# Queries and keys turned unsplit, four heads at once, and placed by DMAs

## The reference

```python
q = einsum('bsh,oh->bso', x, Wq).reshape(b, s, 16, 32)   # 16 query heads, 4 key/value heads, 32 wide
q = q * cos + rotate_half(q) * sin                       # the same for k
k, v = repeat(k, 4), repeat(v, 4)                        # 4 query heads share one key head
attn = softmax(einsum('bhqd,bhkd->bhqk', q, k) * scaling)
out = einsum('bhqk,bhkd->bhqd', attn, v)                 # then Wo
```

## Time and profile before

| | |
|---|---|
| median of three runs | 1792.23 us |
| profiled execution, its own time | 1810.5 us |
| its span, first to last instruction | 1808.7 us |
| mean granted clock of TensorE | 0.970 |
| busy, share of the span | PE 94%, DVE 59%, POOL 55%, ACT 48% |
| DVE, ACT and POOL from 800 to 900 us | 95.45, 88.94 and 90.05 us of 100 |

### The profile page before, as it was taken

How to read it: one execution, slowest core, us unless ns; L and a number is a source line. 1 busy time by engine, 2 the same in 40 slices (tenths; PEclk the granted TensorE clock), 3 DMA queues, 4 the chain that set the end, 5 groups by cost and what they waited for, 6 DMA issues and landing times.

```text
span 1808.7 us, 25064 instructions
## 1 busy us (share of the span) xinstructions
PE 1694.1 (94%) x8596; PEld 1348.5 (75%) x8596; DVE 1067.5 (59%) x1766; ACT 859.3 (48%) x1274; POOL 1001.0 (55%) x775
## 2 busy tenths in 40 slices
PE   6999999999987989999999999888999899999997
PEld 5887899899865766666666666556888689999885
DVE  4554322222567679999999999997645422222226
ACT  4322222232223348898989898873432212232220
POOL 3115574337433439898989899951221519541645
PEclk9999999999988989999999999999999899999998
DMA  9205553333540000000000000003101535533427
GB/s 344 85 28 214 200 182 129 122 121 125 178 131 24 1 1 1 1 1 1 1 1 1 1 1 1 7 18 143 53 1 47 195 122 175 178 123 105 153 87 233
DMA packets 54310, 160.01 MB, mean 88 GB/s; under 512 B 6704, under 2 KB 7600, under 8 KB 51632
## 3 DMA queue, kind: packets, MB, share of 16 engines
q1 hardware_dynamic: 41360, 84.74, 13.4%
q0 software_dynamic: 12832, 73.67, 11.6%
HBM read 102.29 MB, written 55.84 MB: 87 GB/s over the span
## 4 chain that ended last, share of the span: by engine, by line
PE 61%; DVE 17%; ACT 7%; DMA 7%; issue 6%; POOL 1%; SPq 0%; ACTq 0%; DVEq 0%; another core or an unknown queue 0%; POOLq 0%
PE PS L1051 10%; PE PS L1052 10%; PE PS L1053 10%; DVE nmf L1816 5%; DVE Ph L1833 5%; PE PS L1246 4%; DMA xn<-x_routed 3%; ACT Ph L1529 3%; DMA xs<-x_routed 2%; ACT PT L1522 2%; PE PS L1173 2%; PE PS L1178 2%; PE PS L1176 2%; PE PS L1175 2%; PE PS L1177 2%
## 5 line engine op out<-in xcount | busy, mean ns | idle before, releaser
L1980 POOL TENSOR_TENSOR Pl<-PT,Ph 128x1024 fp32r<-128x1024 f32 x176 | 437.4, 2500 | 78.5 <-ACT Ph L1529 73.4
L1816 DVE TENSOR_REDUCE nmf<-PS 128x1 f32<-128x1024 f32 x256 | 307.8, 1213 | 38.7 <-PE PS L1246 36.0
L1522 ACT ACTIVATE PT<-PS 128x1024 f32<-128x1024 f32 x256 | 259.0, 1016 | 19.9 <-DVE Pl L1839 10.3
L1279 PE MATMUL PS<-Ph,V 128*65 128x512 f32 x512 | 207.4, 405 | 10.3 <-DVE Pl L1839 9.9
L1280 PE MATMUL PS<-Pl,V 128*65 128x512 f32 x512 | 203.2, 397 | 0.0
L1529 ACT ACTIVATE Ph<-PT 128x1024 fp32r<-128x1024 f32 x184 | 194.1, 1055 | 1.5
L1888 POOL TENSOR_TENSOR W<-raw,W 128x544 fp32r<-128x544 f32 x144 | 190.1, 1355 | 1.5
L1246 PE MATMUL PS<-KS,QS 96*128 96x512 f32 x512 | 171.4, 416 | 16.3 <-ACT PT L1522 11.7
L1798 DVE TENSOR_TENSOR thid<-thid,PS 128x352 f32<-128x352 f32 x78 | 40.7, 521 | 245.8 <-ACT thid L1445 245.8
L1264 PE MATMUL PS<-QS,KS 98*128 98x512 f32 x512 | 174.8, 423 | 6.0 <-DVE nmf L1816 5.8
L1445 ACT ACTIVATE thid<-PS 128x352 f32<-128x352 f32 x78 | 36.3, 465 | 260.3 <-PE PS L1178 260.3
(11 more groups left out here) (184 smaller groups left out, 4133.1 us busy)
## 6 DMA issues: line engine op xcount, KB each, us to landing
raw<-ffn_w POOLq DMA_DIRECT2D x18, 2176.0 KB, 10.4
y_routed<-ytile SPq DMA_DIRECT2D x78, 256.0 KB, 2.0
xn<-x_routed SPq DMA_DIRECT2D x40, 256.0 KB, 3.2
...
```

The lines of the kernel that those rows point to most:

```text
L1279: e.matmul(PS[0:VCOL, ob, :], V[:, b * QT + kt, g, :], high_part(u)[:, js], start=kt == 0, stop=False)
L1522: e.activation(PT[:, u % PTBUF, :], PS[:, i:i + 2, :].rearrange("p b n -> p (b n)"), ACT.Exp, scale=SCALE).then_inc(p_ready.sem, 1)
L1816: e.tensor_reduce(nmf[:, (n % 3) * REP + h, t:t + 1], PS[:, i:i + 2, :].rearrange("p b n -> p (b n)"), AX.X, ALU.max, negate=True).then_in ...
L1980: e.tensor_tensor(low_part(u)[:], PT[:, u % PTBUF, :], high_part(u)[:], ALU.subtract).then_inc(pl_pool.sem, 1)
```

## The change

Keys and queries are no longer stacked before they are turned. One transpose takes a rotated tile as it is, all four heads at once (128 tokens by 4 x 32 features), and leaves it unsplit in PSUM; four tiles fill a bank of 512 columns. Then ACT copies the bank as high part (128x512) and VectorE subtracts it as low part, and twelve DMAs on SP (four heads, three rows of the stack, 32 partitions by 512 columns, 64 KB each) put the parts into KS or QS. There are 4 such placements of keys, 4 of early queries (groups 0 and 1, at tiles 5, 9, 10 and 12) and 12 of later ones (two per head group 2 to 7, done in groups 0 to 5): 240 DMAs. The parts have one buffer each (early_hi and early_lo, later_hi and later_lo), so that `split_before` lets a split wait for the DMAs of the split before it. kst, TS and their instructions on ACT and POOL go. The row maxima of group 0 start one tile later: none with tile tq = 0, five with tq = 1 to 4, four with tq = 5 to 7. In groups 0 to 6 VectorE takes 3 high parts and 5 low parts of 16 units in place of 4 and 4; ACT thus takes 13 high parts, POOL 11 low parts. Some buffers move (parts, row maxima), with waits of their own at the start of the head stage.

```diff
+def in_last_group(u):
+    return u // UNITS == len(KV_GROUPS) - 1
 def hi_on_vector(u):
-    return u % 4 == 1 or u // UNITS == len(KV_GROUPS) - 1 and u % 4 == 3
+    return u % 4 in (1, 3) if in_last_group(u) else u % 16 in (1, 7, 13)
 def lo_on_vector(u):
-    return u % 4 == 2 or u // UNITS == len(KV_GROUPS) - 1 and u % 4 != 0
+    return u % 4 != 0 if in_last_group(u) else u % 16 in (2, 4, 8, 10, 14)
...
+QUERY_STACK, KEY_STACK = (0, 1, 0), (0, 0, 1)
+EARLY_QUERIES = {5: (0, 0), 9: (0, 1), 10: (1, 0), 12: (1, 1)}
...
+    maxima = [("row_max", 0, h, t) for t in range(QT) for h in range(REP)]
...
-        if tq >= 0:
-            work.append(("turn", *stacked.pop(0)))
...
-            work.append(("turn_keys", PROJECTED[i - 1]))
-        if tq >= 0:
-            work.append(("turn", *stacked.pop(0)))
+            work.extend([("turn_keys", PROJECTED[i - 1]), ("place_keys", ORDER[1])])
         for h in range(REP - 1):
-            if tq >= 0:
-                work.append(("row_max", 0, h, tq))
+            if tq > 0:
+                work.append(maxima.pop(0))
+                if h == 2 and tq <= REP:
+                    work.append(maxima.pop(0))
             if h == 1:
-                work.append(("split_keys", t))
                 beside_step()
+                if i in EARLY_QUERIES:
+                    work.append(("turn_queries", *EARLY_QUERIES[i]))
             work.append(("project", t, h + 1))
+            if i in EARLY_QUERIES and h == 1:
+                work.append(("place_queries", *EARLY_QUERIES[i]))
...
             if i > 0 and tq != 0 and h == 1:
                 work.append(("turn_keys", PROJECTED[i - 1]))
-        if tq >= 0:
-            work.append(("row_max", 0, REP - 1, tq))
-    work.append(("turn_keys", PROJECTED[-1]))
+                if i % TPG == 0:
+                    work.append(("place_keys", PROJECTED[i - 1] // TPG))
+        if tq > 0:
+            work.append(maxima.pop(0))
+    work.extend([("turn_keys", PROJECTED[-1]), ("place_keys", PROJECTED[-1] // TPG)])
...
-        if stacked and pair == 3:
-            work.append(("turn", *stacked.pop(0)))
-        if n + 2 < groups and pair == 1:
-            work.append(("stack", n + 2, un // 4))
-            stacked.append((n + 2, un // 4))
+        if n + 2 < groups and un % (UNITS // 2) == 5:
+            work.append(("turn_queries", n + 2, un // (UNITS // 2)))
+        if n + 2 < groups and un % (UNITS // 2) == 6:
+            work.append(("place_queries", n + 2, un // (UNITS // 2)))
...
+    def split_before(lane, *what):
+        i = early_splits.index(what) if what in early_splits else later_splits.index(what)
+        old = (early_splits if what in early_splits else later_splits)[i - 1]
+        if i and old[0] == "place_keys":
+            lane.wait_ge(keys_placed, *old[1:])
+        elif i:
+            lane.wait_ge(queries_placed[old[1] % 3], *old[1:])
...
+            elif kind == "place_keys":
...
+                sp.wait_ge(keys_hi, g)
+                sp.wait_ge(keys_lo, g)
+                for h in range(NKV):
+                    for i, part_ in enumerate(KEY_STACK):
+                        e.dma_start(KS[i * HD:(i + 1) * HD, b, h, cols].bitcast(F32),
+                                    (early_hi, early_lo)[part_][h * HD:(h + 1) * HD, :]).then_inc(keys_placed.sem, 16)
+            elif kind == "place_queries":
...
+                sp.wait_ge(queries_hi, n, half)
+                sp.wait_ge(queries_lo, n, half)
+                for h in range(REP):
+                    for i, part_ in enumerate(QUERY_STACK):
+                        src = (later_hi, later_lo)[part_] if beside_heads(n) else (early_hi, early_lo)[part_]
+                        e.dma_start(QS[n % 3][i * HD:(i + 1) * HD, h, cols].bitcast(F32),
+                                    src[h * HD:(h + 1) * HD, :]).then_inc(queries_placed[n % 3].sem, 16)
...
         def turn_keys(t):
-            pe.wait_ge(k_lo, t)
...
-            for h in range(NKV):
-                mm = e.transpose(PS[0:STK, KEY_BANK, h * P:(h + 1) * P], kst[:, t % 2, h, :], identf[:])
-            mm.then_inc(k_turned.sem, 1)
-            free[KEY_BANK] = (k_ready, t)
...
+            g, cols = tile_columns(t)
+            pe.wait_ge(k_rotated, t)
+            if t % TPG == 0:
+                until_free(KEY_BANK)
+            e.transpose(PS[:, KEY_BANK, cols], qka[:, t % 2, NH:, :].rearrange("p h d -> p (h d)"),
+                        identf[:]).then_inc(k_turned.sem, 1)
+            free[KEY_BANK] = (keys_lo, g)
+        def turn_queries(n, half):
+            b, g = KV_GROUPS[n]
             until_free(MISC)
-            for h in range(REP):
-                mm = e.transpose(PS[0:STK, MISC, h * P:(h + 1) * P], stack_of(n, t)[:, h, :], identf[:])
-            mm.then_inc(stack_turned.sem, 1)
-            free[MISC] = (stack_ready, n, t)
+            for j in range(TPG):
+                t = b * QT + half * TPG + j
+                pe.wait_ge(q_ready, t)
+                mm = e.transpose(PS[:, MISC, j * P:(j + 1) * P], qtok[:, t, g * REP * HD:(g + 1) * REP * HD], identf[:])
+            mm.then_inc(queries_turned.sem, 1)
+            free[MISC] = (queries_lo, n, half)
...
-            pe.wait_ge(stack_ready, n, t)
-            pe.wait_ge(k_ready, b * QT + QT - 1)
+            pe.wait_ge(queries_placed[n % 3], n, t // TPG)
+            for kg in range(b * NG // B, (b + 1) * NG // B):
+                pe.wait_ge(keys_placed, kg)
...
-                    e.activation(kst[:, i, :, 0:2 * HD].rearrange("p h (c d) -> p h c d", d=HD).bitcast(F32R),
-                                 qka[:, i, NH:, :].unsqueeze(2).broadcast_to([P, NKV, 2, HD]),
-                                 ACT.Copy).then_inc(k_hi.sem, 1)
...
-                e.activation(QS[n % 3][0:STK, :, t * P:(t + 1) * P],
-                             PS[0:STK, MISC, :].rearrange("p (h n) -> p h n", n=P),
-                             ACT.Copy).then_inc(stack_ready.sem, 1)
+            elif kind == "place_keys":
+                g, = key
+                act.wait_ge(k_turned, g * TPG + TPG - 1)
+                act.wait_ge(home_out[ORDER[0]])
+                split_before(act, kind, g)
+                e.activation(early_hi[:].bitcast(F32R), PS[:, KEY_BANK, :], ACT.Copy).then_inc(keys_hi.sem, 1)
+            elif kind == "place_queries":
+                n, half = key
+                act.wait_ge(queries_turned, n, half)
+                split_before(act, kind, n, half)
+                e.activation((later_hi if beside_heads(n) else early_hi)[:].bitcast(F32R), PS[:, MISC, :],
+                             ACT.Copy).then_inc(queries_hi.sem, 1)
...
+            elif kind == "place_keys":
...
+                dve.wait_ge(keys_hi, g)
...
+                split_before(dve, kind, g)
+                e.tensor_tensor(early_lo[:].bitcast(F32R), PS[:, KEY_BANK, :], early_hi[:],
+                                ALU.subtract).then_inc(keys_lo.sem, 1)
+            elif kind == "place_queries":
+                n, half = key
+                hi, lo = (later_hi, later_lo) if beside_heads(n) else (early_hi, early_lo)
+                dve.wait_ge(queries_hi, n, half)
+                split_before(dve, kind, n, half)
+                e.tensor_tensor(lo[:].bitcast(F32R), PS[:, MISC, :], hi[:], ALU.subtract).then_inc(queries_lo.sem, 1)
...
-            elif kind == "stack":
-                n, t = key
...
-                e.tensor_tensor(stack_of(n, t)[:, :, HD:2 * HD].bitcast(F32R), src, stack_of(n, t)[:, :, 0:HD],
-                                ALU.subtract).then_inc(stack_lo.sem, 1)
-            elif kind == "split_keys":
...
```

More of the change, by code:

```diff
@@ L573, in macaron @@
     assert at >= slot_at[3] + slot_bytes
-    OT, _ = place("OT", (P, GRP), F32, at)
+    OT, behind = place("OT", (P, GRP), F32, at)
+    nmf_first, _ = place("nmf_first", (P, REP, QT), F32, behind)
     ropeS, _ = place("ropeS", (P, QT, 2, HD), F32, at)
     qka, at = place("qka", (P, 2, NQK, HD), F32, x_at + ORDER[0] * TPG * D * 4)
-    kst, at = place("kst", (P, 2, NKV, STK), F32, at)
+    early_hi, at = place("early_hi", (P, GRP), F32, at)
     assert at <= x_at + (ORDER[0] + 1) * TPG * D * 4
     qkr, at = place("qkr", (P, 2, NQK, HD), F32, x_at + ORDER[1] * TPG * D * 4)
-    early_TS, at = place("early_TS", (P, 2, REP, STK), F32, at)
+    early_lo, at = place("early_lo", (P, GRP), F32, at)
     assert at <= x_at + (ORDER[1] + 1) * TPG * D * 4
@@ L585, in macaron @@
     assert at <= wqkv_at - NT // 2 * NKV * VCOL * 4 and PROJECTED[QT] == 0
-    TS, at = place("TS", (P, 2, REP, STK), F32, g_at[1] + group_bytes)
-    nmf, at = place("nmf", (P, 3 * REP, QT), F32, at)
+    later_hi, at = place("later_hi", (P, GRP), F32, g_at[1] + group_bytes)
+    later_lo, at = place("later_lo", (P, GRP), F32, at)
     assert at <= g_at[2]
@@ L605, in macaron @@
         at += 2 * GRP * 4
+    parts_at.append(parts_at.pop(7))
+    nmf_later, at = place("nmf_later", (P, 2 * REP, QT), F32, at)
```

(15 more changed lines are left out.)

87 lines of the change are left out of this document (29 added, 58 removed).

## The result

The changed kernel takes 1834.67 us (median of four runs, 1831.82 to 1838.79) against 1792.4: ratio 1.0234, interval 1.0208 to 1.0261, slower. That is 42 us more; the forecast was 1805, and the range ended at 1824. The profiled execution took 1831.98 us, its span is 1830.2.

The account below looks back on a forecast made before the run. VectorE (work, waits for GpSimd, idling: 35.9 us per 16 units) bounds the heads, group 0's row maxima the projection's second half. 1810.5 + 10.3 (projection) + 2 (heads) - 18.3 = 1804.5, said 1805; range 1774 to 1824.

Parts of the forecast that it names:

- The sum of the heads: Head stage: +3.6 in groups 0 to 5, -1.5 in group 6, 0 in the last group; together about +2 us.
- the price of the new shares: Heads, VectorE: one high part becomes low, +0.5 work per 16 units; waits fall from 5.2 to 4.1 us.
- rival 3: Heads, turn: PE waits for VectorE's low part and head, ACT and GpSimd run dry; +27, 1829 with projection; chance 0.09.
- The waits of the parts themselves: Heads, VectorE: mean times including waits for GpSimd near 1.6 us for high parts and 1.4 for low parts.
- I let this 2.0 replace the present 1.8: Heads, VectorE behind the queries' turn: 2.0 us idling replaces the present 1.8; adding it instead would be +1.8 more.
- rival 1: Heads: VectorE and GpSimd parts exclude each other and are the bound; period falls to 34.2, time 1779; chance 0.32.
- The projection: Projection stage: start of chain, chain, tile 12, tile 5 and fewer key transposes sum to +10.3 us, from 0 to +16.
- the stop at tile 12: Projection: queries (1,1) and keys 0 share buffers, so VectorE waits for DMAs and the chain stops; +7.9 (2.9 to 8.4).
- the keys' way to the first matmul: Projection, start of the chain: copy, subtraction, twelve DMA issues at 0.39 and landing take 7.7 us; first reduction +6.9.
- Rival 4: The twelve DMAs are cheap, 2.2 us together, so the projection rises less and the time is 1795; chance 0.11.
- D: Projection: four key transposes become one, kst and ACT copies go; 0 to -6 us, taken as -3.
- The chain itself: Projection's second half, row maxima of group 0: 69.1 us against 71.6 before, -2.5.

Follow-up runs that it names:

- e6: Changed kernel with VectorE's old shares (4 high, 4 low parts of 16 units) and the queries' turn at unit 7 instead of 5; ratio to before 1.0035.
- e1: Changed kernel with VectorE's old shares (4 high, 4 low parts of 16 units), turn left directly behind the store_head; ratio to before 1.0061.
- e2: Kernel before with nothing but the new shares (VectorE: 3 high, 5 low parts of 16 units); ratio to before 1.0123.
- e5: Changed kernel with VectorE's low parts at units 2, 6, 10, 11, 14 instead of 2, 4, 8, 10, 14; single run 1816.84 us, chip with 1809.62 before.
- e3: Changed kernel with the queries' turn at unit 7 of 16 instead of 5 and its placement at 8; ratio to before 1.0115.
- e9: Changed kernel with VectorE's low parts at units 2, 6, 10, 11, 14, turn at unit 7, queries (1,1) at tile 14; ratio to before 0.9912.
- e10: Changed kernel with 2 high, 6 low parts of 16 on VectorE, turn at unit 7, queries (1,1) at tile 14; ratio to before 0.9834.
- e7: Changed kernel with VectorE's old shares, turn at unit 7, and queries (1,1) at tile 14 instead of 12; ratio to before 0.9991.

## Why the prediction was wrong

The sum of the heads failed: it had about +2, and H rose by 22.9. The work removed gave 11.5 back (e6), the turn's place took 9.1 (e1 against e6), and the new shares took 25.4 (e1); two terms of the sum were wrong.

The first is the price of the new shares. The prediction had them at about -0.6 us in each stretch of groups 0 to 5 (0.5 of work more, 1.1 of waits less) and -1.5 in group 6, by counting each part's work and scaling its wait with the number of GpSimd's parts. Alone, in the kernel before, they cost 21.7 (e2). The step left out that a part's place decides who waits for what stands behind it. The text of the change has a low part in front of the store_head at units 5 and 9; at 9 place_max follows one unit later and needs the bank that this head frees. VectorE's order in front of the turn was even shown, and the low part in it (L1886) entered only rival 3. What e1, e2 and e5 show is the place; that it acts through bank MISC is read from PE's waits at place_max, up to 1.4 us with these places (1.7 in e2) and 0.3 with those of e5, and was not tested with a bank of its own. That the clock could fall behind such waits was in no term.

The waits of the parts themselves came out on both sides of the forecast: from 699 to 1115 us the high part has a mean of 1.88 us (forecast 1.6), the low part 1.27 (1.4).

```profile
L2017 POOL TENSOR_TENSOR Pl<-PT,Ph 128x1024 fp32r<-128x1024 f32 x122 | 322.9, 2663 | 94.8 <-ACT Ph L1556 74.0 <-DVE Ph L1878 20.8
L1886 DVE TENSOR_TENSOR Pl<-PT,Ph 128x1024 fp32r<-128x1024 f32 x55 | 69.8, 1270 | 0.0
L1878 DVE CAST Ph<-PT 128x1024 fp32r<-128x1024 f32 x33 | 62.2, 1884 | 0.0
```

GpSimd waits 94.8 us here for high parts, 42.1 before in a stretch of about the same length.

The second is the turn. Its mechanism was right, PE's wait and VectorE's idling of 2.0 (2.16 measured). The balance was not. "I let this 2.0 replace the present 1.8" made it free; it costs 0.82 a turn with the old shares (e1 against e6), 9.1 us, and with the new ones 13.6 by the profile of e3, some 21 with its stretches at the lower clock taken off. Where PE, VectorE and ACT each stand for 2 us one after the other, less work on PE gives nothing back.

In e6, the whole gain of the work removed is seen: heads of 17.50, 35.0 for two, where rival 1 has 35.1 of parts that exclude each other. The trace agrees there with the exclusive port pair of the Trainium skill ("SBUF — State Buffer", section "Who interferes with whom"). The time follows the shares, but not all the way down: e9 takes 34.4 where the parts make 33.2, and e10 33.6 where they make 31.4 and PE is 97% busy. In the changed kernel the shares were not placed so that this floor could be reached, and rival 1 took no account of that.

The projection was forecast at +10.3. A and B, the chain, came to +14.5 from the profiles, of which the chain is 13.3. The terms: the stop at tile 12 was 7.9 by the forecast and is 10.3 (from the end of the queries' low part to that of the keys', 627.64 to 637.98); the keys' way to the first matmul 10.4 and not 7.7. Both mainly by SP's 0.63 for each DMA in place of 0.39. That was a misreading: the 0.78 of the earlier trace rows is one small DMA and not two, and the small ones of the kernel before took 0.63 too. Rival 4, and with it the estimate by a DMA's cost from the Trainium skill ("DMA: Bandwidth & Descriptors", section "Anatomy of one DMA — SWDGE (gpsimd) path"), read as one transfer, is refuted: 8.9 us for the twelve against 3.8. These are twelve issues, and the page's figure is for one DMA, on GpSimd's path. What made up for it is the first half: the keys' last turn ended 62.5 us behind the first projection matmul (513.5 to 576.0), before 71.0 (519.4 to 590.4), -8.5 where D had -3. That this made up for part of the DMAs' cost is luck. The chain itself was put at -2.5, but with the stop moved (e7) B is still 4.3 longer than before. Part of that is the clock: B ran at a mean granted clock of 1.00 in the kernel before, 0.89 in the changed one (the lines below, in this order) and 0.91 in e7. One and the same row maximum came 3.1 us behind the one ahead of it in the changed kernel, at the lower level, and 2.0 in e7, at the higher.

```profile
592.34:661.78 69.44, 63.23 (x331) 48.36 (x330) 52.35 (x72) 22.65 (x52) 22.76 (x39) 1.00 0.00 1
587.64:670.30 82.66, 56.39 (x242) 42.16 (x241) 53.05 (x70) 4.62 (x12) 10.76 (x13) 0.89 0.16 39
```
